# A minGRU and FFN block on one core: the last layer's variances of batches 1 to 6 taken from the fusion units' states, the input rows normalised on GpSimd

## The chip, the cores and the metric

The kernel runs on one core of a Trainium2 chip. The metric is the device time of one execution in microseconds; the time of the kernel before is the median of three runs.

## The reference

Shapes: x is (8, 512, 512), that is 8 batches of 512 tokens with 512 features. Cut to what matters:

```python
def mingru(x, Wz, bz, Wh, bh):            # one layer, one direction
    z = sigmoid(x @ Wz.T + bz); h = tanh(x @ Wh.T + bh)
    return scan(a = clip(1 - z), b = z * h)        # h_t = a_t h_(t-1) + b_t, over tokens

def stack(x):                              # 4 layers, Wz = Wh = ctx[i], bz = bh = cond[i]
    h = x
    for i in range(4):
        new = mingru(h, ...) + (h if i > 0 else 0)
        h = layernorm(new, gamma, beta)    # over the 512 features
    return h

xn = layernorm(x)
f  = stack(xn); g = flip(stack(flip(xn)))           # forward and backward direction
x  = x + concat(f, g) @ fusion_W.T + fusion_b
h  = gelu(layernorm(x) @ ternary(W_fc).T)           # hidden 2048
x  = x + layernorm(h, ln_w, ln_b) @ ternary(W_proj).T
```

Each direction's last layer ends in a layer normalisation over features, so its output needs the variance of each token. The kernel folds the mean into the weights, so that of the last layer only 1/sqrt(variance + eps) of each token and direction is left; it is called `rl`.

## The kernel before, in words

All code is written for five engines by hand: TensorE (PE), VectorE (DVE), ScalarE (ACT), GpSimd (POOL) and SyncE (SP, which issues the DMAs). Each engine works through its own list in order, and semaphores join the lists.

**The recurrence.** `JOBS` lists 56 jobs (batch, direction, layer); layer 0 of both directions is one job, since they share its matmuls. The jobs run in slots `s`: in a slot PE does the four output tiles `mm(k, 0..3)` of one job, each of 12 matmuls of 128x512, and between them transposes. Features lie on partitions (tile `H`, 128 x 4 x 512). To normalise a layer, `tokens` (L519) turns two blocks of 128 tokens, 8 transposes of 128x128, into PSUM banks (`RING`); a direction and layer (a tail) takes two such calls, 16 transposes. DVE's `stats` takes mean and variance (L1132, L1135), POOL's `inv` the power -1/2 (L1597 for the last layer, L1599 to L1603 for the others), ACT's `norm` writes normalised tokens into `ntok` (L849), PE's `back` (L533) turns them again to features, and ACT and DVE write the high and the low part `AH`, `AL` for the next layer's matmuls. The last layer stops after `inv`: only `rl` is kept, and SP stores `H` to memory (`hs_scratch`).

For each batch's layer 0 the input rows `xbuf` are normalised in `norm_x`, on ACT (L863), four instructions of 128x512, at the end of the slot before the batch's. PE's `back("x", ...)` of the tile m = 2 comes in the slot two ahead of the batch's, and all four instructions must be done for it. POOL does in each slot four `keep` (L1578, the clipping of 1 - z), four `add` (L1587, the residual), the `inv` of two halves, and in slots 24 to 55 a piece of the ternary weights (`excess`, L1655 and L1657).

**The FFN.** Then come 128 steps `j`, that is batch b and hidden tile c of 16. In a step PE does `fc(j)` (8 matmuls into `HIDDEN`), `proj` of the step two before (8 matmuls), and in between the fusion of the next batch: a unit `u` is 128 tokens of a batch, and unit 4b+4+i is fused in two halves, `fuse(u, 0)` at c = 2, 5, 8, 11 and `fuse(u, 1)` one step later (12 matmuls each, L572), both into the one bank `PS[2]`. DVE's `resid(u, 0)` reads the first half with `rl` before the second half may be written. `feat(u)` (L585, 4 transposes into the bank `TURNED`) and `moments` use other banks. SP's `load_unit(u)` loads the unit's states `hc` and rows `xr` from memory. ACT turns `hc` into `hch` (`whole`), DVE into `hcl` (`cut`). `spread_sums` on SP sends four rows of constants round through memory; POOL's `whole_row` (at j = 4 and 7) waits for them.

Of the kernel before, what the change touches and what calls it, by code (L numbers as in the profile page):

```python
# [14 lines left out]
NB = 8  # L15
# [29 lines left out]
FUSE_AT = (2, 5, 8, 11)  # L45

# [119 lines left out]
for _s in SLOTS:  # L166
    if _s == SUM_SLOT:
        USERS.append(("M",))
    if _s in ROW_SLOT:
        USERS.append(("G", ROW_SLOT.index(_s)))  # L170
    for _what, _who, _o, _n in RING_SLOT:
        _i = subject(_who, _s - _o)
        if _i is not None and _what == "T":
            USERS += [("T", _i, _n, 0), ("T", _i, _n, 1)]
        elif _i is not None and (_who == "x" or TAILS[_i][2] < 3):
            USERS.append(("x" if _who == "x" else "h", _i, _n))
# [12 lines left out]
STATS = {u: n + 1 for n, u in enumerate(order(START_STAT, STAT_SLOT) + [("h", LAST, 0), ("h", LAST, 1)])}  # L189
INVS = {u: n + 1 for n, u in enumerate(order(START_INV, INV_SLOT) + [("h", LAST, 0), ("h", LAST, 1)])}  # L190
# [27 lines left out]
def pixart_block(nc, x, wt, cond, fwt, fb, gamma, beta, fct, lnw, lnb, pjt, out):  # L218
# [90 lines left out]
    sb(p2, "pad", [128, 336])  # L309
# [16 lines left out]
    glx = sb(p2, "glx", [128, 4, S], F32R)  # L326
# [63 lines left out]
    f_rd = sem("f_rd")  # L390
    f_ma, f_mp = sem("f_ma"), sem("f_mp")
# [26 lines left out]
    def _(e):  # L418
# [84 lines left out]
        def tokens(tau, pr):  # L503

            if tau is None:
                return
# [69 lines left out]
        def feat(u):  # L576
# [76 lines left out]
        def moments(b):  # L653
# [5 lines left out]
            e.wait_ge(f_x1, 8 * min(b + 2, NB))  # L659
            for p, a in ((TURNED, acc), (PS[2], acq)):  # L660
# [147 lines left out]
    def _(e):  # L808
# [121 lines left out]

        def unit_feat(u):
# [111 lines left out]
        for s in SLOTS:  # L1043
# [21 lines left out]
            norm_x(batch(s + 1))  # L1065
# [12 lines left out]
        whole(4)  # L1078
        for j in range(NB * NC):
            b, c = j // NC, j % NC  # L1080
            hidden(j)
            if b > 0 and c == 2:
# [10 lines left out]
    def _(e):  # L1093
# [8 lines left out]
        def scan(k, m):  # L1102
# [21 lines left out]
        def stats(tau, pr):  # L1124
            if tau is None:
                return
# [125 lines left out]

        def resid(u, h):
# [4 lines left out]
            if h == 0:  # L1258
                if t == 0:
# [39 lines left out]
        def low_part(j):  # L1299
# [225 lines left out]
        for j in range(NB * NC):  # L1525
# [3 lines left out]
            low_part(j)  # L1529
            if b > 0 and c == 1:  # L1530
# [33 lines left out]
    def _(e):  # L1564
# [24 lines left out]
        def inv(tau, pr):  # L1589
            if tau is None:  # L1590
# [54 lines left out]

        def excess(n):
# [30 lines left out]
        def addx(u):  # L1677
# [5 lines left out]
            e.tensor_tensor(xr[i][:], xr[i][:], fbb[:], ALU.add).then_inc(f_xf, 1)  # L1683

# [86 lines left out]
        for s in SLOTS:  # L1771
# [14 lines left out]
            keep(job(s - 2), 2)  # L1786
            inv(tail_b(s - 4), 1)
# [33 lines left out]
    def _(e):  # L1821
# [84 lines left out]
        def load_unit(u):  # L1906
# [125 lines left out]
```

## Time and profile before

| | |
|---|---|
| median of 3 runs | 1540.48 us (1540.29 to 1540.55) |
| the profiled execution's own time | 1540.21 us |
| its span (first to last instruction) | 1538.4 us |
| PE busy | 1518.7 us, 99% |
| DVE busy | 1307.8 us, 85% |
| ACT busy | 1021.6 us, 66% |
| POOL busy | 829.6 us, 54% |
| granted TensorE clock | full, but for the first microseconds and the last one |
| DMA | 113.2 MB, 74 GB/s |

The engine with the largest share comes first when reading it; the shares are means over two stages with different work, the recurrence up to about 895 us and the FFN from there.

### The profile page before, as it was taken

To read this page: it belongs to the slowest core of one execution; us is meant where nothing else is said; L and a number is where in the kernel's file an instruction comes from. 1 tells how busy PE (TensorE), PEld (TensorE's weight loads), DVE (VectorE), ACT (ScalarE), POOL (GpSimd) and SP (SyncE) were. 2 spreads that over 40 slices of the span, in tenths; PEclk is the share of its full clock that TensorE was granted. 3 is DMA by queue.
4 is the path that set the end of the run, shared out by engine and by line. 5 is a ranking of instruction groups with operands and counts; after the bars stand their busy time and mean duration, and the time that the engine had idled before them with its cause. 6 is when DMAs were issued, how large, how long until landed. Compare 5 with 4: busy or idle time off the path is not lost.

```text
span 1538.4 us, 22933 instructions
## 1 busy us (share of the span) xinstructions
PE 1518.7 (99%) x7744; PEld 1202.7 (78%) x7744; DVE 1307.8 (85%) x2021; ACT 1021.6 (66%) x1688; POOL 829.6 (54%) x1013
## 2 busy tenths in 40 slices
PE   9999999999999999999999999999999999999999
PEld 7877888888888888888888877777777777777776
DVE  8998999999899989999888887786877777776786
ACT  7988789898687897787987444445454444444354
POOL 6766657578868678676788632331423333332331
PEclk9999999999999999999999999999999999999999
DMA  4211212321312112122044551030302020111000
GB/s 171 76 37 68 103 56 90 124 69 63 123 40 85 56 41 90 65 94 89 29 145 143 193 171 42 1 110 1 96 15 89 22 89 22 62 48 41 29 20 36
DMA packets 73157, 113.20 MB, mean 74 GB/s; under 512 B 5193, under 2 KB 37961, under 8 KB 69970
## 3 DMA queue, kind: packets, MB, share of 16 engines
q1 hardware_dynamic: 72754, 111.21, 21.3%
q8 instruction: 63, 1.03, 0.3%
q14 instruction: 52, 0.43, 0.1%
q10 hardware_dynamic: 288, 0.52, 0.1%
HBM read 73.95 MB, written 37.77 MB: 73 GB/s over the span
## 4 chain that ended last, share of the span: by engine, by line
PE 50%; DVE 2%; ACT 1%; issue 0%; POOL 0%; DVEq 0%; ACTq 0%; POOLq 0%
PE ps L639 15%; PE ps L620 14%; PE ps L572 11%; PE ps L499 6%; PE ps L519 1%; PE ps L585 1%; PE ps L533 1%; PE ps L649 1%; DVE bnp L1132 1%; PE ps L662 0%; ACT H L876 0%; DVE H L1120 0%; DVE yb L1112 0%; ACT AH L880 0%; DVE H L1121 0%
## 5 line engine op out<-in xcount | busy, mean ns | idle before, releaser
L499 PE MATMUL ps<-AH,WH 128*128 128x512 f32 x896 | 366.9, 409 | 7.8 <-DVE H L1121 6.1
L499 PE MATMUL ps<-AL,WH 128*128 128x512 f32 x896 | 351.0, 392 | 0.0
L499 PE MATMUL ps<-AH,WL 128*128 128x512 f32 x896 | 349.4, 390 | 0.0
L1587 POOL TENSOR_TENSOR H<-H,yb 128x512 f32<-128x512 f32 x192 | 245.9, 1291 | 8.5 <-DVE yb L1112 1.3
L1112 DVE TENSOR_TENSOR_SCAN yb<-ab,ps 128x512 f32<-128x512 f32 x192 | 231.9, 1208 | 15.5 <-POOL ab L1578 9.1
L950 ACT ACTIVATE g<-ps 128x512 f32<-128x512 f32 x128 | 76.5, 598 | 248.7 <-PE ps L620 248.7
L837 ACT ACTIVATE yb<-ps,ncnd 128x512 f32<-128x512 f32 x224 | 158.2, 706 | 87.3 <-PE ps L499 84.2
L499 PEld LDWEIGHTS ps<-AH,WH 128*128 128x128 f32 x896 | 168.5, 188 | 46.3 <-DVE H L1121 8.6
L1307 DVE SCALAR_TENSOR_TENSOR gl<-g,wbcol,gh 128x512 fp32r<-128x512 f32 x118 | 116.9, 991 | 97.7 <-ACT gh L960 97.6
L499 PEld LDWEIGHTS ps<-AL,WH 128*128 128x128 f32 x896 | 168.1, 188 | 37.1
L1688 POOL TENSOR_TENSOR rs<-mv,nhalf 128x1 f32<-128x1 f32 x32 | 43.0, 1342 | 282.2 <-DVE mv L1279 282.2
L499 PEld LDWEIGHTS ps<-AH,WL 128*128 128x128 f32 x896 | 169.0, 189 | 29.4
L1132 DVE BATCH_NORM_STATS2 bnp<-ps 128x6 f32<-128x512 f32 x256 | 165.2, 686 | 20.6 <-PE ps L519 20.1
L1578 POOL TENSOR_SCALAR ab<-yb 128x512 f32<-128x512 f32 x224 | 139.8, 624 | 70.7 <-ACT yb L837 56.3
L849 ACT ACTIVATE ntok<-ps,nbp,rsp 128x512 f32<-128x512 f32 x192 | 140.0, 789 | 45.3 <-POOL nbp L1603 45.0
L1100 DVE SCALAR_TENSOR_TENSOR ps<-yb,ps 128x512 f32<-128x512 f32 x224 | 152.2, 679 | 18.5 <-ACT ps L838 18.3
L876 ACT ACTIVATE H<-ps,bet,gam 128x512 f32<-128x512 f32 x192 | 155.7, 811 | 5.3 <-PE ps L533 5.2
L1144 DVE TENSOR_TENSOR AL<-ps,AH 128x512 fp32r<-128x512 f32 x224 | 146.0, 672 | 11.9 <-ACT AH L880 11.6
L880 ACT ACTIVATE AH<-ps 128x512 fp32r<-128x512 f32 x224 | 139.9, 630 | 3.3 <-PE ps L533 3.2
L1599 POOL TENSOR_TENSOR rsp<-mvp,nhalf 128x2 f32<-128x2 f32 x96 | 68.2, 710 | 121.1 <-DVE mvp L1135 119.8
L519 PE MATMUL ps<-ident,H 128*128 128x128 f32 x1024 | 131.3, 273 | 1.6 <-DVE AL L1144 0.9
L519 PEld LDWEIGHTS ps<-ident,H 128*128 128x128 f32 x1024 | 117.7, 140 | 16.2 <-DVE AL L1144 1.8
(193 smaller groups left out, 3230.4 us busy)
## 6 DMA issues: line engine op xcount, KB each, us to landing
hs_scratch<-H SPq DMA_DIRECT2D x16, 1024.0 KB, 5.4
hc<-hs_scratch SPq DMA_DIRECT2D x32, 512.0 KB, 4.4
xr<-in_x SPq DMA_DIRECT2D x32, 256.0 KB, 4.5
out<-ob SPq DMA_DIRECT2D x32, 256.0 KB, 2.2
xbuf<-in_x SPq DMA_DIRECT2D x7, 1024.0 KB, 7.6
RAW<-in_wt SPq DMA_DIRECT2D x16, 256.0 KB, 6.3
stg<-in_fct SPq DMA_DIRECT2D x16, 256.0 KB, 3.2
stg<-in_pjt SPq DMA_DIRECT2D x16, 256.0 KB, 2.9
```

Source lines behind the costliest of these rows:

```text
L499: r = e.matmul(GATE[i % 3][:], w[:, q, m * 128:(m + 1) * 128], a[:, q, :], start=(n == 0), stop=(n == 11))
L519: r = e.transpose(RING[n % 5][:, m * 128:(m + 1) * 128], H[s][:, m, c:c + 128], ident[:])
L572: r = e.matmul(FUSED[u, h][:], a[u % 2][:, q, :], w[:, q, :], start=(n == 0), stop=(n == 11))
L620: r = e.matmul(HIDDEN[j % 2][:], w[q][:, c * 128:(c + 1) * 128], a[b % 2][:, q, :], start=(n == 0), stop=(n == 7))
L639: r = e.matmul(PROJ[t][:], a[BUFFER[j]][:, t * 128:(t + 1) * 128], PJ[c], start=(c == 0 and a is gh), stop=(c == NC - 1 and a is gl))
L837: e.activation(yb[i % 5][:], GATE[c][:], ACT.Sigmoid, bias=ncnd[:, l, m:m + 1], scale=-1.0).then_inc(s_y, 1)
L876: e.activation(H[s][:, m, :], RING[n][:], ACT.Identity, bias=bet[:, m:m + 1], scale=gam[:, m:m + 1]).then_inc(s_h, 1)
L1100: e.scalar_tensor_tensor(GATE[c][:], yb[i % 5][:], 1.0, GATE[c][:], ALU.subtract, ALU.mult, reverse0=True).then_inc(s_p, 1)
L1112: e.tensor_tensor_scan(yb[i % 5][:, rv], ab[c][:, rv], GATE[c][:, rv], 0.0, ALU.mult, ALU.add).then_inc(s_sc, 1)
L1132: e.bn_stats(bnp[:, r, i, 0:6], RING[BANK[u] % 5][:]).then_inc(s_bs, 1)
L1144: e.tensor_tensor(AL[s][:, m, :], RING[BANK[u] % 5][:], AH[s][:, m, :].bitcast(F32), ALU.subtract).then_inc(s_al, 1)
L1587: e.tensor_tensor(H[s][:, m, :], H[s][:, m, :], yb[i % 5][:], ALU.add).then_inc(s_v, 1)
```

## The change

Last-layer tails of batches 1 to 6 (12 of 16 tails) are no longer turned to tokens: `turned(t)` is true only for layers 0 to 2 and for batches 0 and 7. `tokens`, `stats` and `inv` return at once for the others. Their `rl` is computed in the FFN, unit by unit (units 4 to 27), from the states `hc` that the unit loads anyway: ACT squares all of `hc` (`state_squares`), POOL adds the four feature tiles of each direction, of the values and of the squares (`state_sums`, four additions), PE turns the 4 sums of 128x128 (`spread`, 4 transposes into `TURNED`), DVE reduces them and forms the variance (`factors`, a reduction and three small ones), and POOL takes the power (`state_factors`). The tables at the top place these in steps: unit 4b+5 at c = 1 (squares), 2 and 3 (sums) and 4 (spread), and so on; unit 4 is squared and summed ahead of step 0, and spread at step 1.

`norm_x` of batches 2 to 7 moves from ACT to POOL, behind `keep(job(s - 2), 2)`. SP loads a unit's states one unit earlier, apart from its rows.

```diff
+LATE = NU - 4
+def squared_at(b, c):
+    u = 4 * b + {1: 5, 4: 6, 7: 7, 13: 8}.get(c, 4 * NB)
+    return u if u < LATE else None
+def added_at(b, c):
+    u = 4 * b + {2: 5, 5: 6, 8: 7, 14: 8}.get(c, 4 * NB)
+    return u if u < LATE else None
+def spread_at(b, c):
+    u = 4 * b + {(0 if b > 0 else 1): 4, 4: 5, 7: 6, 10: 7}.get(c, 4 * NB)
+    return u if u < LATE else None
+def turned(t):
+    return t[2] < 3 or t[0] in (0, NB - 1)
...
     # tokens (PE), stats (DVE), inv (POOL)
-            if tau is None:
+            if tau is None or not turned(TAILS[tau]):
                 return
...
     # PE: feat(u) and moments(b) also wait for f_hr; new:
+        def spread(u):
+            b, n = (u - 4) // 4, u - 4
+            e.wait_ge(f_hs, 4 * n + 4)
...
+            for k in range(4):
+                r = e.transpose(TURNED[:, k * 128:(k + 1) * 128], hsum[:, k, :], ident[:])
+            r.then_inc(f_ht, 1)
...
             fc(j)
+            if spread_at(b, c) is not None:
+                spread(spread_at(b, c))
...
     # ACT
+            e.activation(hsq[:], hc[i][:], ACT.Square).then_inc(f_hq, 1)
...
             made(s)
-            norm_x(batch(s + 1))
             norm(tail(s - 3), 0)
...
         whole(4)
+        state_squares(4)
...
     # DVE, factors(u), behind low_part(j)
+            e.reduce_sum(htot[:, r, :], TURNED[:].rearrange("p (k n) -> p k n", k=4), axis=AX_X).then_inc(f_hr, 1)
+            e.scalar_tensor_tensor(hmean[:, r, :], htot[:, r, 0:2], 1.0 / 512 ** 2, htot[:, r, 0:2], ALU.mult, ALU.mult)
+            e.tensor_scalar(hve[:, r, :], htot[:, r, 2:4], 1.0 / 512, EPS, ALU.mult, ALU.add)
+            e.tensor_tensor(hvar[:, r, :], hve[:, r, :], hmean[:, r, :], ALU.subtract)
...
     # DVE, resid(u, 0)
+                if 4 <= u < LATE:
+                    e.wait_ge(f_rl, u - 3)
...
     # POOL
+            for i in range(4):
+                e.tensor_scalar(ntok[w % 2][:, i, :], xbuf[:, i, :], rs[:, b % 2, i:i + 1], nb[:, b % 2, i:i + 1], ALU.mult,
+                                ALU.add).then_inc(s_xn, 1)
...
             keep(job(s - 2), 2)
+            norm_x(batch(s + 1))
             inv(tail_b(s - 4), 1)
...
+            e.tensor_tensor(pair, src[:, :, 0:2, :], src[:, :, 2:4, :], ALU.add).then_inc(f_hs, 1)
+            e.tensor_tensor(hsum[:, 2 * of_squares:2 * of_squares + 2, :], pair[:, :, 0, :], pair[:, :, 1, :],
+                            ALU.add).then_inc(f_hs, 1)
...
         addx(4)
+        state_sums(4, 0)
+        state_sums(4, 1)
...
     # SP
+            if u >= 6:
+                e.wait_ge(f_hq, min(u - 5, LATE - 4))
+                e.wait_ge(f_hs, min(4 * (u - 6) + 1, 4 * (LATE - 4)))
...
+        load_states(5)
         for u in range(NU):
             if u == 2:
                 spread_sums()
-            if u + 5 < NU and u + 5 > 4:
-                load_unit(u + 5)
+            if u + 6 < NU:
+                load_states(u + 6)
+            if u + 5 < NU:
+                load_rows(u + 5)
```

Where the operations stand on POOL in the slot ahead of batch 5's first job, before (`ab<-yb` is `keep`, `H<-H,yb` is `add`, `rl<-` the last layer's `inv`, `rsp`, `nmp`, `nbp` the `inv` of a tail that goes on to the next layer):

```order
L1657 TENSOR_TENSOR stg<-raw,stg 128x512 [waits s_pp]
L1587 TENSOR_TENSOR H<-H,yb 128x512 [waits s_h,s_sc]
L1597 TENSOR_TENSOR rl<-mvp,nhalf 128x2 [waits s_ag]
L1578 TENSOR_SCALAR ab<-yb 128x512 [waits s_y]
L1599 TENSOR_TENSOR rsp<-mvp,nhalf 128x2 [waits s_ag]
L1600 TENSOR_SCALAR nmp<-mvp 128x2
L1603 TENSOR_TENSOR nbp<-nmp,rsp 128x2 [waits s_rs,s_nm]
L1587 TENSOR_TENSOR H<-H,yb 128x512 [waits s_h,s_sc]
```

and in the changed kernel, in the same place (line numbers are the changed kernel's):

```order
L1763 TENSOR_TENSOR stg<-raw,stg 128x512 [waits s_pp]
L1682 TENSOR_TENSOR H<-H,yb 128x512 [waits s_h,s_sc]
L1673 TENSOR_SCALAR ab<-yb 128x512 [waits s_y]
L1749 TENSOR_SCALAR ntok<-xbuf,rs,nb 128x512 [waits s_t2,s_xb]
L1749 TENSOR_SCALAR ntok<-xbuf,rs,nb 128x512 x3
L1694 TENSOR_TENSOR rsp<-mvp,nhalf 128x2 [waits s_ag]
L1695 TENSOR_SCALAR nmp<-mvp 128x2
L1698 TENSOR_TENSOR nbp<-nmp,rsp 128x2 [waits s_rs,s_nm]
```

The last layer's `inv` has gone, and the four instructions of `norm_x` stand ahead of the `inv` whose result the next `norm` on ACT needs.

On PE at the start of the FFN, `fc(1)` and `fc(2)` (four rows each) before the first half of unit 4's fusion, before the change:

```order
L620 MATMUL ps<-xh,FCA 128x512 x2
L620 MATMUL ps<-xh,FCB 128x512 x2
L620 MATMUL ps<-xl,FCA 128x512 x2
L620 MATMUL ps<-xl,FCB 128x512 x2
L620 MATMUL ps<-xh,FCA 128x512 x2
```

and after it:

```order
L678 MATMUL ps<-xh,FCA 128x512 x2
L678 MATMUL ps<-xh,FCB 128x512 x2
L678 MATMUL ps<-xl,FCA 128x512 x2
L678 MATMUL ps<-xl,FCB 128x512 x2
L643 MATMUL ps<-ident,hsum 128x128 x4
L678 MATMUL ps<-xh,FCA 128x512 x2
```

The turning of unit 4's sums now stands between `fc(1)` and `fc(2)`. What it waits for is on POOL, where the list at this place reads, in the changed kernel (`xr<-xr,fbb` is `addx(4)`, the two `rl<-` the `inv` of the last tail):

```order
L1692 TENSOR_TENSOR rl<-mvp,nhalf 128x2 [waits s_ag] x2
L1789 TENSOR_TENSOR xr<-xr,fbb 128x512 [waits d_xr1]
L1803 TENSOR_TENSOR hpair<-hc 128x512 [waits f_hs,d_hs3,d_hc0]
L1807 TENSOR_TENSOR hsum<-hpair 128x256 [waits f_hs]
L1803 TENSOR_TENSOR hpair<-hsq 128x512 [waits f_hs,f_hq]
L1807 TENSOR_TENSOR hsum<-hpair 128x256 [waits f_hs]
```

The four additions of unit 4 stand behind `addx(4)`, where before the next instruction was the `inv_1` of unit 4.

## Rows read from the trace of the kernel before

**Rows 1.** Busy us of PE, PEld, DVE, ACT, POOL, then clock, in two windows.

```profile
400.00:600.00 200.00, 197.40 (x1096) 166.03 (x1095) 183.85 (x304) 166.29 (x275) 147.74 (x209) 1.00 0.18 64
...
1200.00:1500.00 300.00, 300.00 (x1363) 220.35 (x1362) 227.84 (x313) 141.43 (x225) 94.21 (x66) 1.00 0.13 40
```

**Rows 2.** PE's waits over the whole span, the longest in total: us, times, longest.

```profile
PE ps L499 <- DVE H L1121: 6.1, 6, 1.3
```

**Rows 3.** PE in order of time (start, us, count last) around one `tokens`, one `feat`.

```profile
501.45 1.03 PE L519 MATMUL ps<-ident,H 128*128 128x128 f32 x8
502.24 0.48 PE L499 MATMUL ps<-AH,WH 128*128 128x512 f32 x1
502.55 0.40 PE L499 MATMUL ps<-AH,WL 128*128 128x512 f32 x1
...
1133.47 0.60 PE L585 MATMUL ps<-ident,n 128*128 128x128 f32 x4
1133.82 0.48 PE L639 MATMUL ps<-PJB,gh 128*128 128x512 f32 x1
1134.14 0.39 PE L639 MATMUL ps<-PJB,gl 128*128 128x512 f32 x1
```

**Rows 4.** In order of time (start, us): PE, POOL and ACT around batch 4's `norm_x`.

```profile
390.90 0.60 PE L533 MATMUL ps<-ident,ntok 128*128 128x128 f32 x4
...
385.56 1.29 POOL L1587 TENSOR_TENSOR H<-H,yb 128x512 f32<-128x512 f32 x1
...
388.22 0.61 POOL L1578 TENSOR_SCALAR ab<-yb 128x512 f32<-128x512 f32 x1
...
386.53 3.00 ACT L863 ACTIVATE ntok<-xbuf,nb,rs 128x512 f32<-128x512 f32 x4
```

**Rows 5.** The same around batch 5's `norm_x`.

```profile
464.91 1.11 PE L533 MATMUL ps<-ident,ntok 128*128 128x128 f32 x8
...
458.64 1.29 POOL L1587 TENSOR_TENSOR H<-H,yb 128x512 f32<-128x512 f32 x1
...
462.67 0.71 POOL L1599 TENSOR_TENSOR rsp<-mvp,nhalf 128x2 f32<-128x2 f32 x1 [0.74 <-DVE mvp L1135]
...
463.86 1.45 ACT L849 ACTIVATE ntok<-ps,nbp,rsp 128x512 f32<-128x512 f32 x2
```

**Rows 6.** One line on POOL: its durations in ns (least, median, most), all instances.

```profile
L1655 POOL TENSOR_SCALAR stg<-raw,th,nth x32: 757/766/771, 368.1 to 831.9; 128x512 f32<-128x512 f32 x32
```

**Rows 7.** PE and POOL in order of time at the start of the FFN.

```profile
897.52 0.81 PE L620 MATMUL ps<-xh,FCA 128*128 128x512 f32 x2
...
907.02 0.47 PE L572 MATMUL ps<-FUH,hch 128*128 128x512 f32 x1 [0.98 <-DVE x L1270]
...
898.27 1.32 POOL L1683 TENSOR_TENSOR xr<-xr,fbb 128x512 f32<-128x512 f32 x1
```

**Rows 8.** PE's first transposes, and the stretch around the clock's fall behind the last matmul.

```profile
1.52 1.75 PE L539 MATMUL ps<-ident 128*128 128x128 f32 x7 [1.52 <-POOL bn L1730]
...
4.35 1.93 PE L539 MATMUL ps<-ident 128*128 128x128 f32 x15
...
1534.58 0.39 PE L649 MATMUL ps<-PJB,gl 128*128 128x512 f32 x1
...
1537.10:1537.20 0.10, 0.00 (x0) 0.00 (x0) 0.00 (x0) 0.00 (x0) 0.00 (x0) 0.87 1.08 410
```

**Rows 9.** DVE and POOL in order of time in the FFN, where they work at once.

```profile
1197.60 3.17 POOL L1712 TENSOR_TENSOR x<-x,cB 128x512 f32<-128x512 f32 x2
...
1199.55 1.77 DVE L1321 TENSOR_TENSOR acc<-acc,g 128x512 f32<-128x512 f32 x1
1201.24 0.68 DVE L1335 TENSOR_TENSOR acq<-acq,sq 128x512 f32<-128x512 f32 x1
```

**Rows 10.** The time in the FFN from `resid(u, 0)` to the second half of its fusion.

```profile
1152.77 0.74 DVE L1270 SCALAR_TENSOR_TENSOR x<-ps,rl,xr 128x512 f32<-128x512 f32 x1
1155.92 0.58 PE L572 MATMUL ps<-FUH,hch 128*128 128x512 f32 x1
```

More of the change, by code:

```diff
@@ L172 @@
         _i = subject(_who, _s - _o)
-        if _i is not None and _what == "T":
-            USERS += [("T", _i, _n, 0), ("T", _i, _n, 1)]
+        if _what == "T":
+            USERS += [] if _i is None or not turned(TAILS[_i]) else [("T", _i, _n, 0), ("T", _i, _n, 1)]
         elif _i is not None and (_who == "x" or TAILS[_i][2] < 3):
@@ L325, in pixart_block @@
     xh.append(sb(p2, "xh1", [128, KC, S], F32R))
-    glx = sb(p2, "glx", [128, 4, S], F32R)
+    with ExitStack() as p4:
+        glx = sb(p4, "glx", [128, 4, S], F32R)
+    with ExitStack() as p5:
+        hsq = sb(p5, "hsq", [128, 8, 128])
+        hpair = sb(p5, "hpair", [128, 4, 128])
+        hsum = sb(p5, "hsum", [128, 4, 128])
+    sb(p2, "under", [128, 4, S])
     gh = [sb(p2, f"gh{i}", [128, S], F32R) for i in range(3)]
@@ L1081, in _ @@
             hidden(j)
+            if squared_at(b, c) is not None:
+                state_squares(squared_at(b, c))
             if b > 0 and c == 2:
@@ L1124, in stats @@
         def stats(tau, pr):
-            if tau is None:
+            if tau is None or not turned(TAILS[tau]):
                 return
@@ L1529, in _ @@
             low_part(j)
+            if spread_at(b, c) is not None:
+                factors(spread_at(b, c))
             if b > 0 and c == 1:
@@ L1589, in inv @@
         def inv(tau, pr):
-            if tau is None:
+            if tau is None or not turned(TAILS[tau]):
                 return
@@ L1644, in inv_x, with norm_x @@
             e.tensor_tensor(nb[:, r, :], nm[:, r, :], rs[:, r, :], ALU.mult).then_inc(s_xb, 1)
+        def norm_x(b):
+            if b is None:
+                return
+            w = NTOK[("x", b)]
+            e.wait_ge(s_xb, b + 2)
+            e.wait_ge(s_t2, max(T2N[(*NTOK_OF[w - 2], m)] for m in range(KC)) + 1)
+            for i in range(4):
+                e.tensor_scalar(ntok[w % 2][:, i, :], xbuf[:, i, :], rs[:, b % 2, i:i + 1], nb[:, b % 2, i:i + 1], ALU.mult,
+                                ALU.add).then_inc(s_xn, 1)
         def excess(n):
@@ L1803, in _ @@
                 inv_2(b - 1)
+            if spread_at(b, c) is not None:
+                state_factors(spread_at(b, c))
+            if added_at(b, c) is not None:
+                state_sums(added_at(b, c), 0)
+            if c > 0 and added_at(b, c - 1) is not None:
+                state_sums(added_at(b, c - 1), 1)
             if j in (4, 7):
@@ L1915, in load_unit @@
             e.dma_start(xr[u % 3][:], x[b, q * 128:(q + 1) * 128, :]).then_inc(d_xr[u % 3], 16)
+        def load_unit(u):
+            load_states(u)
+            load_rows(u)
         for i in (0, 2):
```

76 lines of the change are left out of this document (70 added, 6 removed).

## The prediction

> **What bounds the kernel now.** I read the page's totals first (PE 99% busy), then the busy time by stage, since a mean over two stages says little. In the recurrence PE is busy 197.4 of 200 us and DVE 183.9; in the FFN PE is busy 300 of 300 and DVE 228 [rows 1]. So every TensorE instruction counts in both stages, and nothing done elsewhere counts unless it comes late. Then I read the waits of PE: the largest entry is 6.1 us in 6 waits, all on the double scan of a layer 0 [rows 2]. PE has almost nothing to win back but its own work, and any new wait adds to the time in full. Last I read the timeline at the places where the changed order puts something in front of PE: the slot before each layer 0, the start of the FFN, one FFN batch.
>
> **1. Transposes removed: −20.9 us.** One call of `tokens` is 8 transposes: they start at 501.45, the next matmul at 502.24 (0.79 us), and that one takes 0.31 us to the following start where 0.23 is usual. That is 0.87 us a call, 0.109 a transpose [rows 3]. 12 tails of 16 are 192 transposes: 20.9 us. DVE loses four statistics for each tail, POOL two powers; as DVE is at 92% and PE loses less than DVE does, PE stays the bound, and the gain can be taken in full.
>
> **2. `norm_x` on POOL: +11.0 us of new waits.** ACT takes 3.00 us for the four instructions, from 386.53 to 389.53, and PE turns their result at 390.90 [rows 4], so there were 1.4 us to spare. The last layer's two calls of `tokens` stand just ahead of that point in batches 3 to 7, so PE comes 2 × 0.87 = 1.74 us earlier, at 389.16. POOL's `add` ends at 386.85, `keep` follows (0.61) to 387.5, then the four. The trace has no such instruction on POOL; the nearest row is L1655, also a tensor-scalar of 128x512 with its two scalars read from memory, 766 ns [rows 6]; `keep`, with constants, takes 610 [rows 4]. With 0.77 each they end at 390.6: PE waits 1.5 us. With 0.69 (keep's duration and a gap) it would be 1.2, with 0.85 (a gap behind L1655's duration) 1.9.
>
> The GPSIMD Engine Reference of the Trainium skill, section "Elementwise — side-by-side cycle accounting", gives simple loop bodies on GpSimd about one cycle per element at 1.2 GHz, that is some 0.45 us each, an estimate from the page; by that PE would wait hardly at all for batch 4 and the whole sum would come out some 7 us lower. L1655's row decides here.
>
> Batch 5's place is worse. `add` ends at 459.93, `keep` at 460.6, the four at 463.7, and only then comes the `inv` which in the trace of before began at 462.67 and let `norm` begin at 463.86 [rows 5]. It takes 1.2 us, so `norm` runs from 464.9 to 466.35. PE's second group of four in the row at 464.91 turns its result: it wants it at 464.91 + 0.44 − 1.74 = 463.6. The wait is 2.8 us. The pattern of jobs repeats every two batches: 2 × 1.5 (batches 4, 6) + 2 × 2.8 (5, 7). For batches 2 and 3, whose slots have no ternary pieces on POOL, I take 1.2 each, an estimate below batch 4's. Sum 11.0; by the bounds of 0.69 and 0.85, 9 to 13. ACT's 3 us saved win nothing: no wait of PE depends on them once the rows come from POOL.
>
> **3. Transposes added: +10.6 us.** `feat` has the same form: 0.35 us to the next start and 0.09 more on the first matmul behind it, 0.44 [rows 3]. 24 `spread` are 10.6 us. Each waits for POOL's sums; in batches 1 to 5 these are ready a step or more ahead.
>
> **4. The start of the FFN: +5.9 and +1.5 us.** PE would start `fc(2)` at 897.52 [rows 7]; in the changed order it stops there for unit 4's sums. POOL ends `addx(4)` at 899.59 and then has four additions: 128x512 is 1.29 us, half of it 0.65, estimated from the size; together 3.9, so 903.5 at best. DVE's two-input work of the first steps shares something with them (below); I take 904.4. PE idles 6.9 us. The wait of 0.98 us at 907.02 for a busy DVE [rows 7] disappears, since DVE catches up. Net 5.9; bounds 5.0 and 6.8.
>
> An idle this long also costs clock. The granted clock fell to half at 1537.1 to 1537.2, 2.2 us after PE's last matmul ended (1534.58 + 0.39) [rows 8], so it will fall here. At the start of the program transposes came every 0.21 to 0.22 us, at half rate (1.2 GHz); from about 4.6 us on they are at 0.11 (2.4 GHz) [rows 8]: 3.1 us of work at half rate, a loss of 1.5. Bounds: 0 and 2.5. Nothing hides it.
>
> Behind that, SP's `spread_sums` now waits for `cut(5)` through `load_states(7)`, and POOL's `whole_row` for it, with unit 6's sums queued behind; by my count they are done some 5 us before PE asks. I cost it at nothing; without that cover it would be a wait of a few us.
>
> **5. The FFN's other engines: +3.0 us.** DVE gets a reduction and three small ones a unit, about 1.2 us, priced from the duration of a 128x512 read (0.7) and small ones; its 72 idle us in 300 [rows 1] hold that. But POOL's additions hold up DVE: during two of them (3.17 us) DVE's `acc` takes 1.77 us, and 0.68 when POOL is quiet [rows 9]. The chain that matters is DVE's `resid(u, 0)` before the second half of the fusion: it ends at 1153.51, PE starts at 1155.92, 2.4 us to spare [rows 10]. A unit's four additions are 3.9 us of POOL. Where all fall into one step (unit 4b+5 in step 2, unit 4b+7 in step 8) the slack can be used up. I take 0.5 us for every unit that may be hit, about 6 of them whole: 3. Bounds 0 (DVE always wins) and 9 (0.4 for each of 24).
>
> **Sum.** −20.9 + 11.0 + 10.6 + 5.9 + 1.5 + 3.0 = +11.1. Against the profiled execution's own 1540.2 this is 1551.3; the median of the runs is 0.3 higher, so 1551.6 us. With all low bounds it is +3.7 (1544), with all high ones +22 (1562).
>
> **The rivals.**
>
> *Faster: POOL is in time.* With the last layer's `inv` gone, POOL could reach the rows' four instructions earlier than I place them, and the sums of unit 4 could be ready before PE comes. Then only 1, 3 and 5 are left: −20.9 + 10.6 + 3 = −7.3, or 1533. For it: POOL is busy only 148 of 200 us in the recurrence [rows 1]. Against it: the `add` ahead of them ends at 386.85 and 459.93 without any `inv` before it [rows 4, 5], and at the start POOL's own list is 2 us behind PE before its first addition [rows 7]. It decides as soon as the waits of 2 and 4 stay under 10 us together. Chance 0.15.
>
> *No change: POOL's instruction is short.* At 0.5 us each, batch 4's four end at 389.5 and PE waits 0.35, batch 5's chain ends at 465.25 and PE waits 1.65, batches 2 and 3 not at all: 2 × 0.35 + 2 × 1.65 = 4.0 in place of 11.0, and with no contention in the FFN −20.9 + 4.0 + 10.6 + 7.4 = +1.1, 1541. Against it: both rows of such instructions are longer [rows 4, 6]. Chance 0.10. The Trainium skill's GPSIMD Engine Reference, cited in 2, speaks for this one.
>
> *DVE becomes the bound in the FFN.* The GPSIMD Engine Reference of the Trainium skill, section "Key points", says that GpSimd shares its SBUF interfaces with VectorE and contends with instructions that have two SBUF inputs; rows 9 agree. If each of the 96 additions cost DVE its full duration on a chain without slack, that is 24 × 3.9 = 94 us of DVE against 72 idle in 300: some steps would stretch, by 10 us in place of 3, giving 1559 to 1565. Against: POOL's additions lie in steps where DVE has slack. Chance 0.12.
>
> *The removed transposes are not worth their time*, because DVE (92%) or POOL, now with 3 us more in one slot, paces the recurrence: half the gain, 1562. Against: DVE loses more work than PE. Chance 0.08.
>
> The forecast: 0.55.
>
> **How the numbers follow.** Repeated runs lie within 0.02%, and I take 0.2% (3.1 us) as what can be told from no change. Faster: the first rival, 0.15. Same: the second, and nothing of the forecast's own, 0.10. Slower: 0.75. The range reaches down to the middle of the first rival, 1533, and up to the bounds of the forecast and the DVE rival, 1563; the likeliest case by itself is 1544 to 1562.
>
> **What would show it.** In the profile after: `tokens` x832 in place of x1024; the new transposes x96 behind `fc`. PE waiting for POOL's `ntok` before the rows' transposes in six places of 1 to 2 us, and for ACT's `norm` twice or three times 2 us. One idle of PE of 6 to 7 us after `fc(1)`, with a granted clock of 0.5 for some 3 us behind it. POOL's `norm_x` instruction at 0.77 us. The forecast is wrong first if that instruction is much shorter, if the sums of unit 4 are ready by 898, or if `fuse` waits for DVE in every unit.

## The result, and the profile after

| | before | changed |
|---|---|---|
| median of the runs | 1540.51 us (1540.29 to 1540.70) | 1576.20 us (1574.39 to 1579.92) |
| ratio | | 1.0235, 95% 1.0216 to 1.0253 |
| span of the profiled execution | 1538.4 us | 1572.2 us |
| PE busy, transposes of `tokens` | 99%, x1024 | 97%, x832 |
| DVE, POOL busy | 85%, 54% | 87%, 62% |
| mean granted clock | 1.000 | 0.993 |

The change made the kernel 35.7 us slower. The forecast was 11.1 us slower, 1551.6, with a range up to 1563: the sign was right, the size was not. The profile is of the fastest of the four executions, whose span is 33.8 us longer than before.

PE's waits in the changed kernel, in the form of [rows 2] (us in total, times, longest):

```profile
PE ps L610 <- DVE x L1361: 12.1, 10, 2.0
PE ps L643 <- POOL hsum L1807: 10.3, 2, 6.9
PE ps L571 <- ACT ntok L911: 7.1, 10, 2.0
PE ps L537 <- DVE H L1195: 6.1, 6, 1.3
PE ps L571 <- POOL ntok L1749: 5.2, 5, 1.7
```

Before, the fourth row was the first. The third and the fifth hold the recurrence's new waits (1.8 us of the third, in 7 waits of at most 0.3, were there before), the second the start of the FFN, the first the fusion's second halves (L610), which wait for DVE's `resid` (L1361) twice in each of five batches.

**The recurrence went about as forecast.** Batch 4's and batch 5's places, PE, POOL and ACT in order of time (start, us), against [rows 4, 5]:

```profile
387.17 0.61 POOL L1673 TENSOR_SCALAR ab<-yb 128x512 f32<-128x512 f32 x1
387.88 3.04 POOL L1749 TENSOR_SCALAR ntok<-xbuf,rs,nb 128x512 f32<-128x512 f32 x4
...
390.98 0.65 PE L571 MATMUL ps<-ident,ntok 128*128 128x128 f32 x4 [1.66 <-POOL ntok L1749]
...
459.19 3.05 POOL L1749 TENSOR_SCALAR ntok<-xbuf,rs,nb 128x512 f32<-128x512 f32 x4
462.18 0.73 POOL L1694 TENSOR_TENSOR rsp<-mvp,nhalf 128x2 f32<-128x2 f32 x1
...
463.41 1.45 ACT L911 ACTIVATE ntok<-ps,nbp,rsp 128x512 f32<-128x512 f32 x2 [3.97 <-POOL nbp L1698]
...
462.30 0.66 PE L571 MATMUL ps<-ident,ntok 128*128 128x128 f32 x4 [0.55 <-POOL ntok L1749]
464.91 0.66 PE L571 MATMUL ps<-ident,ntok 128*128 128x128 f32 x4 [1.95 <-ACT ntok L911]
```

The four instructions of `norm_x` take 3.04 us on POOL, end at 390.9 (forecast 390.6), and `inv` and ACT's `norm` follow as written; the waits in batch 5's place are 0.55 and 1.95 us, 2.5 where 2.8 was forecast. The first full `fc` starts at 888.46 where it stood at 895.82: 7.4 us won by here, 9.9 forecast.

**The start of the FFN and one step of a batch:**

```profile
896.25 1.06 POOL L1807 TENSOR_TENSOR hsum<-hpair 128x256 f32<-128x256 f32 x1
...
897.36 1.12 PE L643 MATMUL ps<-ident,hsum 128*128 128x128 f32 x4 [6.85 <-POOL hsum L1807]
...
914.94 0.32 SPq L2034 DMA_DIRECT2D sums_scratch<-ob  x1
...
925.85 3.00 POOL L1835 TENSOR_TENSOR c<-c,ob 128x512 f32<-128x512 f32 x2 [7.24 <-DMA ob<-sums_scratch]
...
934.82 1.12 PE L643 MATMUL ps<-ident,hsum 128*128 128x128 f32 x4 [3.44 <-POOL hsum L1807]
```

The first wait is the forecast one (6.9). The second is not: `spread_sums` leaves SP's queue only at 914.94, `whole_row` (L1835) waits 7.24 us for its DMA, and unit 6's sums, queued behind it on POOL, come 3.4 us after PE wants them.

```profile
1029.31 1.30 POOL L1803 TENSOR_TENSOR hpair<-hc 128x512 f32<-128x512 f32 x1
1030.68 1.07 POOL L1807 TENSOR_TENSOR hsum<-hpair 128x256 f32<-128x256 f32 x1
1031.90 1.53 POOL L1803 TENSOR_TENSOR hpair<-hsq 128x512 f32<-128x512 f32 x1
...
1029.29 1.87 DVE L1400 SCALAR_TENSOR_TENSOR gl<-g,wbcol,gh 128x512 fp32r<-128x512 f32 x1
1031.08 1.23 DVE L1414 TENSOR_TENSOR acc<-acc,g 128x512 f32<-128x512 f32 x1
1032.22 1.75 DVE L1428 TENSOR_TENSOR acq<-acq,sq 128x512 f32<-128x512 f32 x1
1033.90 0.74 DVE L1361 SCALAR_TENSOR_TENSOR x<-ps,rl,xr 128x512 f32<-128x512 f32 x1
...
1030.77 0.71 PE L678 MATMUL ps<-xh,FCA 128*128 128x512 f32 x2
...
1034.78 0.47 PE L610 MATMUL ps<-FUH,hch 128*128 128x512 f32 x1 [1.96 <-DVE x L1361]
```

Here lies the largest part of the miss. While POOL adds, three DVE instructions that take 0.68 to 0.75 us alone take 1.87, 1.23 and 1.75; `resid`, which stands behind them, ends late, and PE stops. It is the same in batches 1 to 5, each time at two places: 0.5 us at the unit fused in steps 5 and 6, 1.95 us at the unit of steps 8 and 9, which is shown here.

**The clock.** Busy time by window (PE, PEld, DVE, ACT, POOL, then the granted clock): the stretches behind the waits at 897, 934 and 1210, and one behind the recurrence's wait at 674:

```profile
897.36:900.10 2.74, 2.74 (x9) 2.03 (x10) 1.94 (x6) 0.00 (x0) 0.27 (x1) 0.50 0.20 73
...
934.30:937.60 3.30, 2.78 (x9) 2.40 (x10) 2.28 (x3) 0.00 (x0) 2.22 (x3) 0.52 0.59 179
674.90:678.20 3.30, 3.30 (x10) 2.59 (x9) 2.81 (x4) 1.90 (x4) 2.97 (x3) 0.52 0.00 0
...
1210.70:1214.10 3.40, 3.40 (x10) 2.61 (x9) 1.86 (x4) 0.45 (x1) 0.00 (x0) 0.53 0.00 0
```

Each is TensorE at 1.2 GHz in place of 2.4. What it costs is half of the part in which PE works: 1.4 us at 897 (the clock had fallen at 893.5, 3.0 us after PE stopped), 1.4 at 934, 1.7 at each of the others. A fifth stood at 1299.6.

**Where the 33.8 us of span lie.** I compare the start of each FFN step with before; from step to step the difference grows only at the places named. The forecast had no term for the last two rows.

| part | forecast | measured |
|---|---|---|
| up to the first full `fc` | -9.9 | -7.4 |
| 24 `spread`, 0.43 each | +10.6 | +10.4 |
| unit 4's sums: wait, less the 0.98 regained, and clock | +7.4 | +7.4 |
| unit 6's sums: wait and clock | 0 | +5.1 |
| waits for `resid`, 5 batches of 2.9 | +3.0 | +14.4 |
| clock behind two of these | 0 | +3.2 |
| rest | | +0.7 |

### The profile page after: what moved, and what is told of

It is laid out like the page before. It is cut to its first block and busy times, and to the rows that moved or that the text cites. A ratio compares the mean times of both kernels' runs of the same rounds, so it can differ in the third digit from the quotient of the medians.

```text
span 1572.2 us, 23050 instructions
## 1 busy us (share of the span) xinstructions
PE 1520.4 (97%) x7648; PEld 1196.1 (76%) x7648; DVE 1360.1 (87%) x2021; ACT 1028.4 (65%) x1688; POOL 976.1 (62%) x1133
## 3 DMA queue, kind: packets, MB, share of 16 engines
q1 hardware_dynamic: 72754, 111.21, 20.9%
q8 instruction: 62, 1.02, 0.3%
## 5 line engine op out<-in xcount | busy, mean ns | idle before, releaser
L1400 DVE SCALAR_TENSOR_TENSOR gl<-g,wbcol,gh 128x512 fp32r<-128x512 f32 x118 | 122.7, 1039 | 66.0 <-ACT gh L1032 65.4
L1218 DVE TENSOR_TENSOR AL<-ps,AH 128x512 fp32r<-128x512 f32 x224 | 146.3, 674 | 16.5 <-ACT AH L942 16.3
L1206 DVE BATCH_NORM_STATS2 bnp<-ps 128x6 f32<-128x512 f32 x208 | 134.3, 686 | 17.9 <-PE ps L557 17.7
L900 ACT ACTIVATE ps<-ps,cnd 128x512 f32<-128x512 f32 x192 | 130.5, 680 | 0.0
L571 PE MATMUL ps<-ident,ntok 128*128 128x128 f32 x880 | 112.5, 275 | 13.0 <-ACT ntok L911 7.1
```

Source lines behind the costliest of these rows:

```text
L900: e.activation(GATE[c][:], GATE[c][:], ACT.Tanh, bias=bias[:, l, m:m + 1]).then_inc(s_t, 1)
L1206: e.bn_stats(bnp[:, r, i, 0:6], RING[BANK[u] % 5][:]).then_inc(s_bs, 1)
L1218: e.tensor_tensor(AL[s][:, m, :], RING[BANK[u] % 5][:], AH[s][:, m, :].bitcast(F32), ALU.subtract).then_inc(s_al, 1)
```

## The experiments

Each kernel ran against the kernel before on the same chip; medians in us. The kernel before had a median of 1540.37 to 1540.52 in all of them, so the times can also be compared with the changed kernel's 1576.20. "Theory A" is: every wait of PE counts in full, at its own place. "Theory B", the rival, is: the added load of DVE and POOL sets the pace, wherever it stands.

**1. `norm_on_act`: the changed kernel with `norm_x` back on ScalarE.**

```diff
     # ACT
             made(s)
+            norm_x(batch(s + 1))
     # POOL
-            norm_x(batch(s + 1))
```

> The changed kernel with the rows of batches 2 to 7 normalised on ScalarE again, as before the change. Theory A (every wait of TensorE counts in full, and a long one costs clock besides): TensorE waited 12.3 us before the transposes of ntok, 2.0 in the kernel before; about 10 of it goes, and with it one fall of the clock, 1.7 us: 11 to 12 us faster than the changed kernel, 1563 to 1565. In theory B (VectorE and GpSimd are loaded too much as a whole, and TensorE's waits only show where this comes out) GpSimd loses 18.6 us of work in the recurrence only, which has slack there: 0 to 4 us faster.

Measured: 1568.88 (1567.11 to 1569.56), 7.3 less than the changed kernel, between what the two theories expected. Moving `norm_x` costs 7.3 us beside the other parts, not 11.0, for two reasons. The wait for ACT's `norm` in odd batches stays, 1.83, 1.46 and 1.45 us; with `norm_x` on POOL it is 1.36, 1.95 and 1.95. It comes from the removed transposes: PE reaches the norm's result 1.7 us earlier and ACT does not. And one clock fall of 1.7 us stays. The first full `fc` now stands 13.8 us earlier than before.

**2. `norm_alone`: the kernel before with only `norm_x` moved to POOL.** The edit is the reverse of the one above, in the kernel before.

> The kernel before with nothing but the rows of batches 2 to 7 normalised on GpSimd; the last layer's variances stay in the recurrence. Theory A: TensorE comes 1.74 us later to each of these places than in the changed kernel, so most of the wait is hidden by the transposes that stand ahead of it: batches 4 and 6 wait 0 to 0.4, 5 and 7 about 1.1, 2 and 3 about 1: 3 to 5 us slower than the kernel before, 1543 to 1546. Theory B: as GpSimd has slack in the recurrence, no change, 1540.5 with 1 either way.

Measured: 1557.02 (1554.69 to 1557.85), ratio 1.0105 (1.0090 to 1.0120). I missed by 12 us. In the profile PE waits for POOL's `ntok` 0.90, 1.12 and 0.91 us in the even batches, and for ACT's `norm` 1.95, 1.96 and 1.96 in the odd ones (I expected about 1, 0.4, 0.4 and about 1.1 each), with one fall of the clock. POOL's list in an even batch:

```profile
393.46 0.70 POOL L1596 TENSOR_TENSOR rl<-mvp,nhalf 128x2 f32<-128x2 f32 x1 [0.57 <-DVE mvp L1134]
394.24 0.61 POOL L1577 TENSOR_SCALAR ab<-yb 128x512 f32<-128x512 f32 x1
394.96 3.02 POOL L1653 TENSOR_SCALAR ntok<-xbuf,rs,nb 128x512 f32<-128x512 f32 x4
```

The last layer's `inv` (L1596) still stands ahead of the four and waits for DVE; in the changed kernel it is gone. That holds in the odd batches too, so PE's later arrival hides little. Without the removed transposes the move costs 16.5 us, with them 7.3: the two parts of the change are not independent. `norm_on_act` shows most of the difference: with the transposes gone and nothing moved, PE already waits 4.7 us in the odd batches and loses 1.7 to the clock.

**3. `late_spread`: unit 4's transposes and factors later in the FFN's first steps.**

```diff
-    u = 4 * b + {(0 if b > 0 else 1): 4, 4: 5, 7: 6, 10: 7}.get(c, 4 * NB)
+    u = 4 * b + {(0 if b > 0 else 2): 4, 4: 5, 7: 6, 10: 7}.get(c, 4 * NB)
...
     # PE: behind proj(0); DVE: behind squares
+            if j == 2:
+                spread(4)
```

> The changed kernel with unit 4's sums turned behind proj(0) in step 2, not behind fc(1), and reduced behind step 2's squares. Theory A: TensorE comes 6.3 us later and finds the sums nearly ready (0 to 1 us), then waits some 1.3 for the fusion's first half; the 6.9 us wait and the 6.8 us at half clock go: 5 + 3.4 = 8 to 9 us faster than the changed kernel, 1566 to 1568. If the clock's fall had not been a loss of its own: 5 us faster. Theory B: no change in the load, so the time comes back later in the FFN: 0 to 2 us faster.

Measured: 1576.16 (1574.54 to 1577.02), no gain: Theory A missed by 8 to 10 us, and Theory B's 0 to 2 came true. The wait for the sums shrank to 0.4 us, and another took its place:

```profile
901.62 0.68 DVE L1333 TENSOR_REDUCE htot<-ps 128x4 f32<-128x512 f32 x1
...
903.71 0.75 DVE L1363 SCALAR_TENSOR_TENSOR x<-ps,rl,xr 128x512 f32<-128x512 f32 x1 [0.87 <-POOL rl L1818]
...
904.60 0.77 PE L610 MATMUL ps<-FUH,hch 128*128 128x512 f32 x1 [4.83 <-DVE x L1363]
```

POOL's sums were there at 897.3, but DVE reaches the reduction only behind the low parts, totals and squares of two steps, as the edit placed it; from there the chain by DVE's factors, POOL's power and `resid` takes 3.0 us more, until PE starts at 904.60. The edit moved PE's and DVE's part together, so it does not show what moving PE's part alone would give. The profiled execution also had one fall of the clock more than the changed kernel's. The load is unchanged and so is the time, which by itself would fit Theory B; what decides between the two is the next experiment.

**4. `sums_wait`: POOL's sums of a unit held until the former unit's `resid`.** This delays POOL and takes no work away.

```diff
             else:
                 e.wait_ge(d_hc[u % 2], 16 * (u // 2) + 16)
                 if n == 0:
                     e.wait_ge(d_hs[3], 64)
+                else:
+                    e.wait_ge(f_x1, 2 * u - 1)
```

> The changed kernel with one wait more: GpSimd begins the additions of a unit (5 to 27) only when VectorE has read the first half of the fusion of the unit before it. The work is the same. Theory A: the additions no longer hold up VectorE's accumulations ahead of resid, so the waits of fuse for VectorE (12.1 us) fall to 0 to 3 and the clock's falls in the FFN's steady part go (3.4 us): 11 to 15 us faster than the changed kernel, 1560 to 1565; spread must still find its sums ready. Theory B: VectorE and GpSimd do as much as before, the collisions only move: 0 to 4 us faster, or slower where spread then waits for the sums.

Measured: 1565.07 (1563.71 to 1566.96), 11.1 less. The row for `resid` in PE's waits:

```profile
PE ps L610 <- DVE x L1361: 2.7, 5, 0.6
```

It was 12.1 in 10, and the FFN's two falls of the clock in the steady part are gone. The same additions, begun some 3 us later and so beside DVE work that PE waits for less soon, cost 11.1 us less. Theory B's load is unchanged here, so the load alone is not what costs. The slack is not back, though: `resid` now ends 0.3, 0.15 and 0.15 us ahead of PE's second half in three of the four units of a batch (the last with the wait of 0.5 to 0.6 us), where the kernel before had 2.2, 2.4 and 1.8.

**5. `sp_order`: `spread_sums` one unit earlier in SP's list.**

```diff
-            if u == 2:
+            if u == 1:
                 spread_sums()
```

> The changed kernel with one line moved: SP issues spread_sums one unit earlier (u == 1), ahead of load_states(7), so it no longer waits behind that load for cut(5). Theory A (each wait of PE costs its length, a long one also clock): whole_row on POOL no longer waits 7.2 us for its DMA, unit 6's sums come in time, PE's wait of 3.4 us at 935 before the transposes of unit 6 and the 1.7 us of half clock behind it go: about 1571, 5 us less than the changed kernel. Theory B (the sum of DVE's and POOL's work in the FFN's first steps sets the pace, not the place of one DMA): the wait moves to the next fuse, and the time stays within 1.5 us of 1576.

Measured: 1571.03 (1570.71 to 1573.06), 5.2 less. `sums_scratch<-ob` goes out at 904.73, and `whole_row` and unit 6's first sum follow without an idle:

```profile
904.73 0.29 SPq L2034 DMA_DIRECT2D sums_scratch<-ob  x1
...
920.55 3.00 POOL L1835 TENSOR_TENSOR c<-c,ob 128x512 f32<-128x512 f32 x2
923.63 1.61 POOL L1803 TENSOR_TENSOR hpair<-hc 128x512 f32<-128x512 f32 x1
```

PE's second wait for `hsum` is gone. This is the cover that I had costed at nothing.

**6. `filled`: the wait for unit 4's sums filled with 60 transposes of the identity.**

```diff
     # PE, in spread(u)
+            if n == 0:
+                e.wait_ge(f_xh, u)
+                e.wait_ge(f_xl, u)
+                for i in range(60):
+                    e.transpose(TURNED[:, 0:128], ident[:], ident[:])
```

> The changed kernel with 60 extra transposes of the identity on PE in place of the idle before the transposes of unit 4 (they write the PSUM tile that those overwrite, so the result is the same). The wait itself, 6.85 us, is as long as before, only filled. Theory A: what an idle costs beyond its length is the clock. The half clock at 893 (6.83 us, 3.4 us of work lost) is gone, nothing else moves: about 1573, 3 us less. Rival: the half clock that the records show costs nothing, or it comes from somewhere else, such as POOL's and DVE's load: still 1576.

Measured: 1574.88 (1573.79 to 1577.48), 1.3 less, with the runs of both overlapping: inconclusive as a time. The trace tells more. The clock stays up at 893, and the waits and clock that follow are:

```profile
890.50:900.00 9.50, 9.15 (x75) 8.14 (x74) 9.06 (x12) 4.09 (x7) 7.14 (x7) 1.00 0.27 85
934.20:940.90 6.70, 6.00 (x16) 4.55 (x16) 4.41 (x9) 0.12 (x1) 4.55 (x5) 0.50 0.37 119
...
907.14 0.47 PE L610 MATMUL ps<-FUH,hch 128*128 128x512 f32 x1 [0.90 <-DVE x L1366]
...
934.90 1.12 PE L648 MATMUL ps<-ident,hsum 128*128 128x128 f32 x4 [3.93 <-POOL hsum L1812]
```

The next `fc` is 1.3 us earlier than in the changed kernel, so that is what the low clock cost there; I expected 3 because I took half of the whole stretch, idle part included. It is then given back: 0.90 in a wait for `resid`, 0.5 more in the wait for unit 6, whose sums depend on SP and POOL and come at the same time as before. Behind that wait the low clock lasted 6.7 us in place of 3.3.

**7. `all_three`: edits 1, 4 and 5 together.**

> The changed kernel with the three single edits together: the rows' normalisation back on ScalarE (norm_on_act, -7.3 us by itself), the first sums of a unit's states held until resid(u-1, 0) (sums_wait, -11.1) and spread_sums one unit earlier (sp_order, -5.2). Theory A (waits in series at different places of PE's list add up): 1576.2 - 23.6 = 1552.6, within 2 us. Rival (the waits hide one another, so each single edit already took what all together can): 1558 or more.

Measured: 1550.40 (1549.86 to 1552.26), 25.8 less than the changed kernel where the single edits give 23.6. It is still 10 above the kernel before; the wait for unit 4's sums, 6.85, is still there. The waits are in series and add up; they do not hide one another.

**8. `from8`: the rows on ScalarE, the new variances only from batch 2 on, the sums held.** Batch 1 keeps its `tokens`, so no unit has to be summed while the FFN starts.

```diff
+EARLY = 8
-    return u if u < LATE else None
+    return u if EARLY <= u < LATE else None
...
-    return t[2] < 3 or t[0] in (0, NB - 1)
+    return t[2] < 3 or t[0] in (0, 1, NB - 1)
```

> A combination: the rows' normalisation back on ScalarE, the last layer's variances from the units' states only for batches 2 to 6 (units 8 to 27; batch 1 keeps its tokens), and the first two sums of each unit's states on POOL held until resid(u-1, 0). By theory A: 20 calls of tokens away (-17.4), 20 of spread added (+8.8), two waits of 1.46 for ScalarE's norm in batches 5 and 7 (+2.9), one wait of 0.55 in each of five FFN batches (+2.8), no wait at the FFN's start: -2.9 against the kernel before, 1537.6; with a clock fall or two up to 1541. Theory B (DVE and POOL pace the FFN): 1550 or more, since five sixths of the added work remains.

Measured: 1541.57 (1541.09 to 1542.31), ratio 1.0006 (0.9998 to 1.0015): 1.05 us more than before, which the interval does not tell from none. Theory A expected 1537.6 and missed by 4. The first full `fc` comes 13.3 us earlier, and the FFN's steps give back 15.2: 20 `spread` are 8.7; of the rest, 0.8 a batch lies at the wait for `resid` (0.54 to 0.58 by the record), and 0.35 a batch at step 7, where PE comes to unit 4b+6's sums just before they are ready (0.14 by the record). Five sixths of the FFN's added work are there and the time is within 0.1% of that of before; Theory B's 1550 is ruled out.

**9. `from8n` and 10. `from8o`: ScalarE's order.** `from8n` puts `norm(tail_b(s - 4), 1)` ahead of `gates(job(s - 2), 3)` in every slot, `from8o` only where PE waited (shown):

```diff
             norm(tail(s - 3), 0)
+            if batch(s + 1) in (5, 7):
+                norm(tail_b(s - 4), 1)
             gates(job(s - 2), 3)
-            norm(tail_b(s - 4), 1)
+            if batch(s + 1) not in (5, 7):
+                norm(tail_b(s - 4), 1)
```

> As the combination from8, and ScalarE does norm(tail_b(s-4), 1) ahead of gates(job(s-2), 3) in each slot. By theory A the 1.46 us waits for that norm in batches 5 and 7 shrink by the two gate instructions (about 1.1 us) and the time is 2 us below from8's. Rival: the gates come 1.5 us later in all 60 slots, DVE's scan follows them, and PE waits for the scan in place of the norm: 1545 or more.

> As from8, and only in the two slots where from8 leaves PE waiting 1.47 us for ScalarE's norm (the slots ahead of batches 5 and 7) does ScalarE do norm(tail_b(s-4), 1) ahead of gates(job(s-2), 3). In from8n, where all slots have that order, these two waits were 0.71 and three new ones of 1.4 us came in other slots. Theory A: 2 x 0.76 = 1.5 us less than from8, 1540.0. Rival (the gates' delay comes back at the next scan in these slots too): 1541.5 or more.

Measured: `from8n` 1543.52, ratio 1.0020 (1.0011 to 1.0029); the two waits fell from 1.47 to 0.71, and three of 1.4, also for ACT's `norm`, appeared at 334.80, 542.10 and 749.11. Neither expectation was met. `from8o` 1539.88 (1539.45 to 1540.52), ratio 0.9997 (0.9988 to 1.0006): 1.7 less than `from8`, as expected.

**11. `from8a` and 12. `from8s`: where POOL's four `add_c` stand.** `from8a` has them at steps 11 to 14 in place of 10 to 13, `from8s`, shown, at 4, 7, 11 and 12.

```diff
-            if b < NB - 1 and 10 <= c < 14:
-                add_c(4 * b - 10 + c)
+            steps = (10, 11, 12, 13) if b == 0 else (4, 7, 11, 12)
+            if b < NB - 1 and c in steps:
+                add_c(4 * b + steps.index(c))
```

> As from8o, and POOL's four add_c of an FFN batch stand at steps 11 to 14 in place of 10 to 13, so that one, not two, of them lies beside DVE's total and squares ahead of resid(u, 0) of the fourth unit. Theory A: the wait of 0.57 us for resid, once in each of five batches, goes: 2.9 us less than from8o, 1537.1, and 0.2% under the kernel before. Theory B (the total of POOL's additions paces DVE, wherever they stand): no change against from8o, or a new wait before the next unit's spread.

> As from8o, and from batch 1 of the FFN on POOL's four add_c stand at steps 4, 7, 11 and 12 in place of 10 to 13: one beside each place where two had delayed DVE, and one fewer ahead of the next batch's sums, which came 0.64 us late in from8a. Theory A: neither the wait of 0.5 us for resid (from8o) nor that of 0.64 for the sums (from8a) is left in batches 2 to 6: 2.5 us less than from8o, 1537.4. Theory B (DVE and POOL together pace the FFN): another wait of half a microsecond a batch appears at the units of steps 4 and 7, and the time stays at 1540.

Measured: `from8a` 1540.27, the same as `from8o`. The wait for `resid` is gone, and the next unit's sums, one addition later on POOL, make PE wait 0.64 in its place:

```profile
1128.54 1.73 POOL L1850 TENSOR_TENSOR x<-x,cB 128x512 f32<-128x512 f32 x1
1130.24 1.74 POOL L1810 TENSOR_TENSOR hpair<-hsq 128x512 f32<-128x512 f32 x1
1132.06 1.06 POOL L1814 TENSOR_TENSOR hsum<-hpair 128x256 f32<-128x256 f32 x1
...
1133.17 0.66 PE L646 MATMUL ps<-ident,hsum 128*128 128x128 f32 x4 [0.64 <-POOL hsum L1814]
```

`from8s` 1547.36 (1546.80 to 1547.62), 7.5 more than `from8o` with the same instructions: three waits in a batch, of 0.6, 0.4 and 0.9. Both expectations of Theory A (1537.1 and 1537.4) failed, and `from8a` came out as Theory B had it: no change, and a new wait before the next unit's transposes. Neither had the 1547 of `from8s`. Theory B as worded, the load wherever it stands, is refuted all the same: the place of four additions is worth 7.5 us. What it has right is that the FFN's added work has used up the slack, so that each order that I tried only moved the wait; Theory A's forecasts had left that out. No version beats the kernel before by what can be told.

## Why the prediction was right or wrong, point by point

The direction was right, and every wait was at a place that the prediction had looked at. The size was not: 35.7 us where 11.1 was forecast. What failed is part 5 of the prediction, the FFN's contention, put at 3.0 us and measured at 14.4 with 3.2 of clock behind it. Beside it stands the wait for unit 6's sums in part 4, put at nothing and measured at 5.1.

1. *Transposes removed, -20.9.* Right. In `norm_on_act` the starts of the recurrence's matmuls come forward against before at 24 places, by 0.79 to 1.02 us each, 20.1 in all; waits and one clock fall take back some 7, and the first full `fc` is 13.8 us early.
2. *`norm_x` on POOL, +11.0.* The instruction (0.775 against 0.77), the order and batch 4's wait (1.66 against 1.5) were right. (The forecast's own numbers give 390.6 - 389.16 = 1.4; batches 2 and 3 came out at 0.93 and 1.36 against 1.2 each.) PE's waits at L571 sum to 12.3 us, where before they were 2.0. What I had put to the moved rows alone is partly the price of the removed transposes, since ACT's `norm` waits for DVE's statistics in any case: by experiment 1 the split is 7.3 for the move. The clock fall at 674.9 (1.7) was not in the sum.
3. *Transposes added, +10.6.* Right: 0.43 each, from the starts of the FFN's steps.
4. *The start.* The wait, 6.9, was right to 0.05, in part by luck: POOL ended `addx(4)` 1.7 us behind PE's arrival, not 2.1, and the four additions took 5.1 us, not 4.8. The clock's 1.5 came out at 1.3 to 1.4, by `filled`. What failed is the sentence "by my count they are done some 5 us before PE asks. I cost it at nothing". I had named SP's `spread_sums` and POOL's queue behind it, and not followed the times: the sums were done 3.4 us after PE asked, and `sp_order` puts 5.2 us on it.
5. *The FFN's contention, +3.0 with bounds 0 to 9.* This part failed, and it carries most of the error: 14.4 us of waits and 3.2 of clock. Its premise was right, [rows 9, 10]: DVE slowed from 0.68 to 1.77, and 2.4 us of slack. The sum was not carried out. Four additions are 1.52 + 1.07 + 1.56 + 1.07 = 5.2 us of POOL in the FFN, not 3.9, because the addition of 128x256, which I took at half of 128x512, takes 1.065 on average and both sizes are slowed too. They slow three DVE instructions ahead of `resid`, by 1.1 + 0.5 + 1.1 = 2.7, and DVE has the new factors of 1.1 us before them. That is 3.8, and a third part is needed: what is left over from the unit before. One of DVE's instructions of step 7 against the `fc` of that step, first in the kernel before and then in the changed one:

```profile
1011.17 0.69 DVE L1277 BATCH_NORM_STATS2 bn<-x 128x6 f32<-128x512 f32 x1
1011.50 0.62 PE L620 MATMUL ps<-xh,FCA 128*128 128x512 f32 x2
...
1021.23 0.69 DVE L1368 BATCH_NORM_STATS2 bn<-x 128x6 f32<-128x512 f32 x1
1019.98 0.61 PE L678 MATMUL ps<-xh,FCA 128*128 128x512 f32 x2
```

It stood 0.3 us ahead of the `fc` and now stands 1.3 behind, 1.6 us of lag from the additions and factors of the steps before. With 0.3 us of idle that DVE gives up, `resid` comes 1.6 + 1.1 + 2.7 - 0.3 = 5.1 us later, counted from the `fc` of step 7. PE takes 2.7 of that: the slack of 2.4, of which 0.15 passes between `resid`'s end and PE's start even when PE waits, and the 0.46 by which the new transposes delay PE. The other 2.4 are the wait, 1.95 by the record and 2.2 by the steps' starts. It falls once in a batch, at the unit of step 8, and 0.5 (0.7 by the starts) at that of step 5; step 2, which the prediction also named, has no recorded wait, but there too the slack is gone: `resid` of that unit ends 0.15 us ahead of PE. The forecast took 0.5 us for about 6 units; it was 10 units, with 0.7 and 2.2 us in turn.

```profile
L1807 POOL TENSOR_TENSOR hsum<-hpair 128x256 f32<-128x256 f32 x48 | 51.1, 1065 | 3.8
...
L1803 POOL TENSOR_TENSOR hpair<-hsq 128x512 f32<-128x512 f32 x24 | 37.5, 1564 | 2.7
L1803 POOL TENSOR_TENSOR hpair<-hc 128x512 f32<-128x512 f32 x24 | 36.5, 1523 | 0.2
L1749 POOL TENSOR_SCALAR ntok<-xbuf,rs,nb 128x512 f32<-128x512 f32 x24 | 18.2, 775 | 0.6
```

Of the rivals, "DVE becomes the bound in the FFN" (1559 to 1565) came nearest. Its picture of a chain without slack, on which some steps stretch, is what happened in the steps 5 to 9; the total of DVE's load is not what did it, by `sums_wait`, `from8` and `from8s`, and DVE still idles 10 to 12 us of the changed kernel's 88 to 89 us in a batch. Its sum set 94 us of DVE against 72 idle in 300; but the 24 units lie in six batches, about 500 us, with some 120 idle. In the forecast's bounds the high ones add up to +21, not +22, which changes nothing. "POOL is in time" fell with the waits of the recurrence and of unit 4, "POOL's instruction is short" with the row of L1749. The rule of about one cycle an element, from the Trainium skill's GPSIMD Engine Reference (section "Elementwise — side-by-side cycle accounting"), about 0.45 us for such an instruction by my estimate, does not fit the 775 ns here. The same section of the Trainium skill also gives about 1.8 cycles an element for a tight unrolled loop, 769 ns measured for 512 elements, which the prediction did not use, and that one fits. The Trainium skill's GPSIMD Engine Reference, section "Key points", that GpSimd contends with VectorE instructions that have two SBUF inputs, agrees with the rows here: DVE's accumulations take 0.68 us alone and 1.2 to 1.8 beside POOL's additions.

Which of the two-microsecond waits is followed by a clock fall stays open: of the changed kernel's five waits of 1.95 in the FFN two were, in `sp_order` three. The changed kernel's runs spread over 5.5 us, where the kernel before has 0.4, and the slowest of them has the lowest mean clock (0.990 against 0.992 and 0.993); that a varying number of falls makes the spread is likely and not shown.

## What to carry to other kernels

When work is added to an engine beside which the one that feeds the bound runs slower, list the instructions between the last point at which that one idles and the one that is waited for, over several steps if it does not idle in between, give each its slowed duration, and hold the sum against the slack of that place; the engine's total share does not show it. A step moved in a DMA queue is followed by times, instruction by instruction, to whoever waits for it last, however many queues lie between. And an addition that is early but not urgent is best held back until the chain that it would disturb has passed: that one wait took back 11 of 36 us.

## What the runs showed that I had not expected

- A wait costs more than the idle that the profile records. Between the start of the `fc` at 1030.77 and the fusion at 1034.78 lie 4.01 us; in the kernel before it is 1.70 from such an `fc`, behind a `feat`, to the fusion (median of 19 records). That is 2.3 us for a recorded 1.96. A part of it is that a matmul recorded at 0.39 us is followed by the next start after 0.23, so that its recorded end lies behind the point where the next could have started.
- POOL's addition of half the size takes 0.73 to 0.75 us alone and 1.06 beside DVE, that of 128x512 1.28 and up to 1.75. The slowing is mutual.
- From 100 us on, no wait of 1.7 us or less was followed by a fall of the granted clock in any run here; of those of 1.83 to 1.96 us some were, and all of 3.4 us and more.
